# Layer 0's up products of the later chunks as three fp32r terms, and two of layer 1's roundings two slots on

## Time and profile before

| | |
|---|---|
| executions, us | 623.47, 627.16, 627.70 |
| median, us | 627.16 |
| profiled execution: span from first to last instruction, us | 622.5 |
| PE busy in it, us | 601.4 (97%) |
| PE weight loads busy, us | 562.2 (90%) |
| DVE, ACT, POOL busy, us | 345.9, 287.3, 111.0 |
| share of the last-ending chain: PE, DVE, ACT | 83%, 10%, 3% |
| granted clock of TensorE, mean | 0.995 |

### The profile page before, as it was taken

How to read it: one execution, slowest core, us unless ns; L and a number is a source line. 1 busy time by engine, 2 the same in 40 slices (tenths; PEclk the granted TensorE clock), 3 DMA queues, 4 the chain that set the end, 5 groups by cost and what they waited for, 6 DMA issues and landing times.

```text
span 622.5 us, 12422 instructions
## 1 busy us (share of the span) xinstructions
PE 601.4 (97%) x4526; PEld 562.2 (90%) x4526; DVE 345.9 (56%) x1221; ACT 287.3 (46%) x955; POOL 111.0 (18%) x328
## 2 busy tenths in 40 slices
PE   8889999999999999999999999999999999999896
PEld 7678788889999999999999999999989899898895
DVE  4865655765464454455553563158947764766314
ACT  3275645645655455455564556546813332311110
POOL 3034121111111111111111110000201321412310
PEclk8999999999999999999999999999999999999899
DMA  8998000000000000000000000090202002003000
GB/s 260 338 311 134 2 1 2 2 2 1 2 2 1 2 1 2 2 2 1 2 1 1 2 2 2 19 185 15 91 1 103 6 5 103 5 5 107 5 1 8
DMA packets 47477, 26.98 MB, mean 43 GB/s; under 512 B 28424, under 2 KB 42680, under 8 KB 46904
## 3 DMA queue, kind: packets, MB, share of 16 engines
q1 hardware_dynamic: 45392, 25.71, 15.2%
q10 hardware_dynamic: 2024, 0.48, 0.4%
HBM read 25.61 MB, written 0.57 MB: 42 GB/s over the span
## 4 chain that ended last, share of the span: by engine, by line
PE 83%; DVE 10%; ACT 3%; issue 2%; POOL 0%; DVEq 0%; POOLq 0%
PE Y L1371 33%; PE U L1371 30%; PE HH L1371 8%; PE ZR L1371 7%; PE M L1371 5%; DVE acc_a L814 2%; ACT gated L648 1%; DVE acc_b L814 1%; DVE rh L814 1%; DVE rank L846 1%; DVE cmp_a L806 0%; DVE fresh L814 0%; ACT cand L626 0%; POOL scaled_lo L566 0%; DVE cmp_b L806 0%
## 5 line engine op out<-in xcount | busy, mean ns | idle before, releaser
L1371 PE MATMUL Y<-l_dn,gated 128*128 128x128 f32 x1152 | 162.7, 284 | 1.8 <-DVE acc_a L814 0.9
L1371 PEld LDWEIGHTS Y<-l_dn,gated 128*128 128x128 f32 x1152 | 141.1, 192 | 3.3 <-issue 2.0
L648 ACT ACTIVATE gated<-U,b1T 128x256 f32<-128x256 f32 x256 | 106.8, 473 | 0.0
L1371 PE MATMUL U<-l_x_hi,l_up_hi 128*128 128x256 f32 x256 | 82.8, 323 | 0.0
L630 ACT ACTIVATE h<-ZR,rnn_b 128x8 f32<-128x8 f32 x128 | 34.3, 268 | 90.5 <-PE ZR L1371 88.1
L814 DVE SCALAR_TENSOR_TENSOR fresh<-zr_s,cand 128x8 f32<-128x8 f32 x128 | 21.4, 167 | 94.6 <-ACT cand L626 92.1
L1371 PE MATMUL U<-l_x_hi,l_up_lo 128*128 128x256 f32 x256 | 72.0, 281 | 0.0
L1371 PE MATMUL U<-l_x_lo,l_up_hi 128*128 128x256 f32 x256 | 72.0, 281 | 0.0
L550 POOL TENSOR_SCALAR zh<-zr_s 128x8 f32<-128x8 f32 x128 | 25.8, 202 | 251.5 <-ACT zr_s L622 251.5
L626 ACT ACTIVATE cand<-HH 128x8 f32<-128x8 f32 x128 | 22.7, 178 | 96.3 <-PE HH L1371 96.3
L1371 PE MATMUL U<-scaled_hi,l_up_hi 128*128 128x256 f32 x192 | 58.8, 306 | 1.7 <-POOL scaled_lo L566 1.7
(11 more groups left out here) (263 smaller groups left out, 1201.5 us busy)
## 6 DMA issues: line engine op xcount, KB each, us to landing
l_bc<-dw SPq DMA_DIRECT2D x4, 1536.0 KB, 6.4
stage<-L_ffn_W_dram SPq DMA_DIRECT2D x4, 768.0 KB, 10.8
w_raw<-L_ffn_W_dram SPq DMA_DIRECT2D x12, 256.0 KB, 6.6
l_up_raw<-L_ffn_W_dram SPq DMA_DIRECT2D x1, 2048.0 KB, 10.0
l_up_raw<-L_ffn_w_dram SPq DMA_DIRECT2D x1, 2048.0 KB, 14.8
l0f_up<-L_ffn_w_dram SPq DMA_DIRECT2D x1, 768.0 KB, 7.0
l0f_dn<-L_ffn_w_dram SPq DMA_DIRECT2D x1, 768.0 KB, 8.4
x<-x_dram SPq DMA_DIRECT2D x1, 512.0 KB, 4.2
```

The costliest lines, as they stand in the source:

```text
L648: last = nc.scalar.activation(gated[:, n % 4, h * N:(h + 1) * N], U[n % 2][:, h * N:(h + 1) * N], ACT.Gelu, bias=b1T[:, col:col + 1])
L1371: return nc.tensor.matmul(out, lhsT, rhs, start=start, stop=stop, skip_group_check=shared)
```

## The change

Chunks 2 and 3 of stream C, and chunks 1 to 3 of stream F, take their up products as three fp32r terms (`mm3`), as layers 1 and 2 do; the first chunks stay float32. These are 12 C units and 18 F units. For that:

- ScalarE makes six rounded weight parts of 128 x 512 in slots 3, 4, 5, 10, 11 and 12 (`l0_high_part`);
- GpSimd makes the six lo parts (`l0_low_part`), each in the place of the raw weights, so after these were read last, and the hi and lo parts of xT for chunks 2 and 3 early on; layer 1's eight lo parts are woven with them, the last four between the keep steps of GRU steps 0 to 3;
- VectorE makes, at chunk 1, 2 and 3's `take_sums`, a hi and a lo part of the scaled sum ahead of c0, for which it still makes the float32 copy (the router and the order of the rest use it);
- TensorE waits for these parts at the first units that use them;
- layer 1's first two hi parts move from slots 8 and 9 to 10 and 12.

```diff
--- before.py
+++ after.py
@@ -59,8 +59,12 @@
 SIG_SLOT = [AT["C", 5, k] + 5 for k in range(CHUNKS)]
 SIG_SLOT[2] = AT["C", 5, CHUNKS - 1] + 1
 SIG_LATE = SIG_SLOT[1]
+L0_SPLIT_X = CHUNKS - 2
+L0_LAST_RAW = [AT["C", 1, 1], AT["C", 3, 1], AT["F", 1, 0], AT["F", 3, 0], AT["F", 5, 0], AT["C", 5, 1]]
+L0_HI_SLOTS = [3, 4, 10, 11, 12, 5]
+L0_HI_ORDER = sorted(range(6), key=lambda j: L0_HI_SLOTS[j])
 GELU_AGAIN = AT["F", 5, 1], A_START - 2
-UP_HI_SLOTS = [8, 9] + [14 + e for e in range(E - 2)], [A_START + 4 + 2 * e for e in range(E)]
+UP_HI_SLOTS = [10, 12] + [14 + e for e in range(E - 2)], [A_START + 4 + 2 * e for e in range(E)]
 W1_SLOTS = [AT[stream, i, k] for k in (1, 2) for stream, i in zip("AAABBB", (7, 9, 11, 7, 9, 11))]
 
 
@@ -241,6 +245,12 @@
 
         with ExitStack() as raw:
             stage = sb("stage", [P, E3 * F], scope=raw)
+            with ExitStack() as first:
+                l0_w13_hi = sb("l0_w13_hi", [P, 2, 2 * P], F32R, scope=first)
+                l0_up_hi = sb("l0_up_hi", [P, E, P], F32R, scope=first)
+                l0f_up_hi = sb("l0f_up_hi", [P, 12 * P], F32R, scope=first)
+                l0_x = [sb(f"l0_x{i}", [P, 2, N], F32R, scope=first) for i in range(2)]
+                l0f_x = [sb(f"l0f_x{i}", [P, 2, N], F32R, scope=first) for i in range(2)]
             l3_up_turned = sb("l3_up_turned", [P, E3, F], scope=raw)
         l3_up_hi = sb("l3_up_hi", [P, E3, F], F32R)
         l3_up = (l3_up_hi, sb("l3_up_lo", [P, E3, F], F32R))
@@ -271,15 +281,20 @@
 
 
         with ExitStack() as early:
-            l0_up = sb("l0_up", [P, E, P], scope=early)
+            with ExitStack() as raw:
+                l0_up = sb("l0_up", [P, E, P], scope=raw)
+                l0_w13 = sb("l0_w13", [P, 2, 2 * P], scope=raw)
+            l0_up_lo = sb("l0_up_lo", [P, E, P], F32R, scope=early)
+            l0_w13_lo = sb("l0_w13_lo", [P, 2, 2 * P], F32R, scope=early)
             l0_dn = sb("l0_dn", [P, E, D], scope=early)
-            l0_w13 = sb("l0_w13", [P, 2, 2 * P], scope=early)
             l0_w2 = sb("l0_w2", [P, 2, D], scope=early)
             silu = sb("silu", [P, 512], scope=early)
             act = sb("act", [P, 512], scope=early)
             gru_c = sb("gru_c", [P, 3 * D], scope=early)
             relu = sb("relu", [P, 2, 512], scope=early)
-            l0f_up = sb("l0f_up", [P, 12 * P], scope=early)
+            with ExitStack() as raw:
+                l0f_up = sb("l0f_up", [P, 12 * P], scope=raw)
+            l0f_up_lo = sb("l0f_up_lo", [P, 12 * P], F32R, scope=early)
             l0f_dn = sb("l0f_dn", [P, 12, D], scope=early)
             gru_w = sb("gru_w", [P, 3, D], scope=early)
             gru_u = sb("gru_u", [P, 3, D], scope=early)
@@ -353,6 +368,7 @@
         e_full, ga_full, gd_full = sem("e_full"), sem("ga_full"), sem("gd_full")
         l3_hid = sem("l3_hid")
         set_up = sem("set_up")
+        l0_hi, l0_lo, l0_x_split, l0f_x_split = sem("l0_hi"), sem("l0_lo"), sem("l0_x_split"), sem("l0f_x_split")
         l0_sig, silu_done = sem("l0_sig"), sem("silu_done")
         gru_zr, gru_gates, gru_rh = sem("gru_zr"), sem("gru_gates"), sem("gru_rh")
         gru_hh, gru_cand, gru_h, gru_keep = sem("gru_hh"), sem("gru_cand"), sem("gru_h"), sem("gru_keep")
@@ -420,6 +436,17 @@
 
             return (scaled_all, POOL_FIRST.index(j) + 1) if j in POOL_FIRST else (scaled_odd, (j - 1) // 2)
 
+        def l0_weights(tiles, j):
+
+            w13, w_up, f_up = tiles
+            if j == 0:
+                return w13[:, :, :].rearrange("p i n -> p (i n)")
+            if j in (1, 5):
+                return w_up[:, at(4 * (j == 5), 4), :].rearrange("p e h -> p (e h)")
+            return f_up[:, at(512 * (j - 2), 512)]
+
+        l0_raw, l0_high, l0_low = (l0_w13, l0_up, l0f_up), (l0_w13_hi, l0_up_hi, l0f_up_hi), (l0_w13_lo, l0_up_lo, l0f_up_lo)
+
         def bank_of(*name):
 
             return M[m_of(*name) % 2]
@@ -523,6 +550,20 @@
                                    base=0, pattern=[[1, n], [-1, n]], channel_multiplier=0).then_inc(consts, 1)
 
 
+            pool.wait_ge(x_rest, 2)
+            for i in range(2):
+                src = xT[:, at((L0_SPLIT_X + i) * N, N)]
+                own(nc.gpsimd.tensor_copy(l0_x[i][:, 0, :], src))
+                nc.gpsimd.tensor_tensor(out=l0_x[i][:, 1, :], in0=src, in1=l0_x[i][:, 0, :], op=ALU.subtract).then_inc(l0_x_split, 1)
+
+            def l0_low_part(j):
+
+                pool.wait_ge(l0_hi, L0_HI_ORDER.index(j) + 1)
+                pool.wait_ge(u_full, L0_LAST_RAW[j] + 1)
+                nc.gpsimd.tensor_tensor(out=l0_weights(l0_low, j), in0=l0_weights(l0_raw, j), in1=l0_weights(l0_high, j),
+                                        op=ALU.subtract).then_inc(l0_lo, 1)
+
+            l0_low_part(0)
             pool.wait_ge(m_free, m_of("mid", 1) + 1)
             pool.wait_ge(zeros, 5)
             own(nc.gpsimd.tensor_tensor(out=pair_bias[:, 3 * D:], in0=pair_bias[:, 3 * D:], in1=cond_pair[:, :], op=ALU.add))
@@ -534,13 +575,24 @@
             nc.gpsimd.tensor_scalar(gru_u[:, 2, :], gru_u[:, 2, :], 0.5, None, ALU.mult).then_inc(gru_scaled, 1)
 
             pool.wait_ge(gru_scaled, 1)
-            for e in range(E):
+
+            def l1_low_part(e):
+
                 pool.wait_ge(up_hi, e + 1)
                 if e:
                     pool.wait_ge(up_split[0], e)
                 nc.gpsimd.tensor_tensor(out=l1_up_lo[:, e, :], in0=l1_up_raw[:, e, :], in1=l1_up_hi[:, e, :],
                                         op=ALU.subtract).then_inc(up_split[0], 1)
-            pool.wait_ge(up_split[0], E)
+
+            l0_low_part(1)
+            l1_low_part(0)
+            l0_low_part(2)
+            l1_low_part(1)
+            l0_low_part(3)
+            l0_low_part(4)
+            l1_low_part(2)
+            l0_low_part(5)
+            l1_low_part(3)
 
             def gru_keep_of(step):
                 h = h_gru[:, at((step - 1) % (2 * CT) * B, B)]
@@ -552,6 +604,8 @@
 
             for step in range(T):
                 gru_keep_of(step)
+                if step < E - 4:
+                    l1_low_part(4 + step)
 
             pool.wait_ge(y_full, DOWNS.index(AT["F", 5, CHUNKS - 1]) + 1)
             for t in (spread[:, :, :], third[:, :, :]):
@@ -691,6 +745,17 @@
                         if l == 1:
                             sc.wait_ge(y_full, DOWNS.index(AT["C", 5, CHUNKS - 1]) + 1)
                     nc.scalar.activation(up[l][0][:, e, :], (l1_up_raw, l2_up_raw)[l][:, e, :], ACT.Copy).then_inc(up_hi, 1)
+
+            def l0_high_part(n):
+                if n in L0_HI_SLOTS:
+                    j = L0_HI_SLOTS.index(n)
+                    if j == 0:
+                        sc.wait_ge(ld_w13, 16 * W13_LOADS)
+                    if j == 1:
+                        sc.wait_ge(ld_l0, 16 * L0_LOADS)
+                    if j == 2:
+                        sc.wait_ge(ld_l0f, 16 * L0F_LOADS)
+                    nc.scalar.activation(l0_weights(l0_high, j), l0_weights(l0_raw, j), ACT.Copy).then_inc(l0_hi, 1)
 
             def scaled_first_high(j):
                 sc.wait_ge(weighted_full, j + 1)
@@ -740,6 +805,7 @@
                     if quarter == 3 and n != SIG_LATE:
                         square_l0(n)
                     if quarter == 3:
+                        l0_high_part(n)
                         up_high(n)
             for n in range(A_START, SLOTS):
                 steps, rnn = gru_steps(n), rnn_steps(n)
@@ -1052,7 +1118,12 @@
                 if (stream, i, k) == ("C", 5, 0):
                     dve.wait_ge(m_free, m_of("mid", 2) + 1)
                 if (stream, i) == ("C", 5):
-                    ts(c0[k % 2][:, :], taken("c", k)[:, 0:N], 1.0 / 3.0, ALU.mult).then_inc(m_free, 1)
+                    m = taken("c", k)[:, 0:N]
+                    if k:
+                        parts = l0f_x[k % 2]
+                        own(ts(parts[:, 0, :], m, 1.0 / 3.0, ALU.mult))
+                        stt(parts[:, 1, :], m, 1.0 / 3.0, parts[:, 0, :], ALU.mult, ALU.subtract).then_inc(l0f_x_split, 1)
+                    ts(c0[k % 2][:, :], m, 1.0 / 3.0, ALU.mult).then_inc(m_free, 1)
                 if (stream, i) == ("F", 5):
                     tt(x1[:, at(k * N, N)], xT[:, at(k * N, N)], taken("f", k)[:, 0:N], ALU.add).then_inc(m_free, 1)
                 stream, i, k = unit(n - 5)
@@ -1491,8 +1562,15 @@
                         cols = at((2 * i + h) % Q * P, P)
                         last = mm3(u, [w[:, i // 2, cols] for w in up[stream == "B"]],
                                    [x[:, :] for x in (l1_x, l2_x)[stream == "B"]], True, True)
+                    elif stream == "F" and k:
+                        cols = at((2 * i + h) * P, P)
+                        last = mm3(u, [w[:, cols] for w in (l0f_up_hi, l0f_up_lo)], [l0f_x[k % 2][:, side, :] for side in range(2)], True, True)
                     elif stream == "F":
                         last = mm(u, l0f_up[:, at((2 * i + h) * P, P)], c0[k % 2][:, :])
```

(14 more changed lines are left out.)

## The result

The changed kernel took 655.8 us (median; 650.9 to 660.5), the kernel before 625.3 beside it: ratio 1.050 [1.046, 1.053]. The forecast of 627.7 and its range of 622 to 631 were wrong, and every case of the prediction with them: the highest rival stood at 630.9. The ratios leave out executions over 1.5% longer than the shortest of the same kernel, which show a lower granted clock; the medians and the clocks in the table keep them.

A forecast was written before the change was run, and what follows sets the result against it. It took the GRU recurrence to be as much the bound as TensorE in slots 20 to 43. Terms -0.3 - 0.6 - 0.3 - 0.4 + 0 + 0.2 + 0.3 + 1.6 gave +0.5 on 627.16: 627.7 us, range 622 to 631.

The forecast's parts named there:

- the highest rival: Slots 7 to 23: GpSimd's new work slows VectorE, 0.17 us an overlap; 630.9 us, chance 0.14.
- the first part of the change: Three fp32r terms per float32 half, 0.08 us less each; in slots 20 to 43 mostly more waiting, -0.3 us.
- Three terms: Shorter TensorE halves: -0.3 us in slots 18 and 19, -0.6 in 60 to 63, -0.3 in 20 to 43.
- Roundings moved: Slot 8: ScalarE's wait for the l1_dn load goes, so the first F unit and all behind come earlier, -0.4 us.
- ScalarE's hi parts: Slots 3 to 5 and 10 to 12: six new roundings fit in gaps or cover, cost 0, at most 1.2 us.
- GpSimd's lo parts: Subtractions slow overlapping VectorE operations by 0.17 us each; +0.2 early on, +0.3 between keep steps of GRU steps 0 to 3.
- The third rival: Slots 7 to 23: GpSimd's subtractions slow VectorE at many overlaps of 0.17 us; 630.9 us, chance 0.14.
- The splits: Slots 21, 33 and 39: two VectorE operations ahead of c0 delay fresh and the gate products, +1.6 us.
- TensorE sets the time throughout: GRU stretch: the loop shortens with TensorE's work, so the saving counts in full; 622.2 us, chance 0.12.
- half a record: All 60 halves: each term costs half a float32 record, if the loop gives way too; 620.3 us, chance 0.03.
- The landing of l1_dn: Slot 8: a late load makes the slower runs and the change removes that; 624.0 us, chance 0.13.
- The sign that the prediction named for its third rival: A GRU stretch longer than before by over 3 us would show GpSimd's work slowing VectorE.

The follow-up runs named there:

- e13: Changed kernel with layer 0's lo parts subtracted by VectorE and layer 1's subtractions ahead of the keep steps; 657.4 us, ratio 1.045.
- e14: As e13, with the first of the three terms issued twice in slots 20 to 43; 628.2 us, ratio 1.006.
- e1: Kernel before with only layer 1's first two roundings moved to slots 10 and 12; 626.1 us, ratio 1.0024.
- e5: Changed kernel with float32 products from rounded weights, no GpSimd layer-0 or x subtractions, layer 1's ahead of the keep steps; 625.2 us, ratio 1.0024.
- e10: Changed kernel with layer 1's subtractions ahead of the keep steps and the first term issued twice in slots 20 to 43; 637.9 us, ratio 1.019.
- e2: Changed kernel with all parts still made, but float32 products from the rounded weights; 637.5 us, ratio 1.020.
- e7: Changed kernel with all three terms from existing hi parts, without GpSimd's layer-0 subtractions or VectorE's splits; 647.8 us (637.4 to 667.2).
- e8: As e7, with the first term issued twice, four records a half; 626.2 us, ratio 1.003.
- e4: Kernel before, float32, with the 30 units' up products on 192 of 256 columns; 639.8 us, ratio 1.000 from four of ten executions.

## Why the prediction was wrong

**What failed** is the first part of the change, in the sentence "In most steps it only turns into more waiting for rh or h_gru". The half did get 0.08 us shorter, and the loop did stay the bound: 29.0 us against 29.1 for thirteen steps. But the waiting isn't free. It was costed at -0.3 with 0 as its bound on the other side; it measured +24 to +29 (e13 against e14), since with less to stream in each step TensorE loses half its clock and is then slower than the loop, 3.4 to 4.4 us a step against 2.0 to 3.1. No part and no rival had the granted clock in it, though a PEclk line stands on the page of before. The bound of 0 had no row behind it; it took for granted that more slack can't hurt. The waits for rh and h_gru, which the prediction expected to grow from 10 to 12 to 14 us, shrank to 4.3.

Point by point:

1. *Three terms.* Slots 18 and 19: a unit takes 1.60 us (53.18 to 54.78) where the float32 unit of slot 16 takes 1.75; -0.15 a unit, as said. From the start of slot 60 to that of slot 64: 12.42 us (205.55 to 217.97) against 12.86 before: -0.4, said -0.6. Slots 20 to 43: above.
2. *Roundings moved.* In e1 the wait went and the F unit came 0.41 earlier, as predicted, and it was lost two slots on (in the changed kernel this unit starts at 34.20, behind a first short fall of the clock at 30.2). "In slots 10 to 14 one overlap goes and one comes" was the wrong sentence: two came, and held VectorE for 1.0 and 0.6 us. Net, e1: +0.2%, not -0.4 us.
3. *ScalarE's hi parts* cost little. e5, which has them, the splits and x's copies, is 0.24% [0.04, 0.43] over before.
4. *GpSimd's lo parts.* +0.5 forecast, 10 to 12 us measured where the terms don't cover it (e14 to e10; e5 to e2). The third rival had the right place and, in "small operations may wait for a whole one", the right mechanism, but priced each overlap at the 0.17 of the earlier trace rows, an overlap with the last 0.30 us of a subtraction; 0.8 to 1.0 is what a fresh, cmp_b or relu paid. Even at that price the overlaps come to a few us: up to the GRU's step 1 the changed kernel is 2.9 behind e7, which lacks them (59.02 and 56.07), short falls of the clock included. The rest is the clock in the GRU's steps. That a long list of subtractions also makes GpSimd's own keep late (e10, above) was in no part.
5. *The splits.* 0.42 for each of the two operations, near the 0.42 and 0.46 taken:

```profile
L876 DVE TENSOR_SCALAR l0f_x<-M x3: 425/425/425, 65.7 to 150.3; 128x256 fp32r<-128x256 f32 x3
L880 DVE SCALAR_TENSOR_TENSOR l0f_x<-M,l0f_x x3: 424/424/425, 66.1 to 150.8; 128x256 fp32r<-128x256 f32 x3
```

   At full clock steps 1 to 32 took 72.0 us with them (e14) and 70.9 without (e8): +1.1, said +1.6.

Of the rivals, "TensorE sets the time throughout" is refuted by the thirteen steps above; "half a record" by the 0.15 a unit. The landing of l1_dn wasn't what makes slower runs: e1 has the room and isn't faster. The sign that the prediction named for its third rival, a GRU stretch longer by over 3 us, did appear (103.9 against 70.2), for another reason than the rival's.

What stays open: what sets off a single fall (that of 30 us, that of 44), why e4 falls in some executions and not in others and e7's take from 637.4 to 667.2 us, and the 1.7 to 3.7 us that e8 and e14 keep over before at a full clock. A kernel that pads its GRU steps by other means than a repeated product wasn't tried, nor one with float32 products beside VectorE's lo parts, for which e14 stands in.

## What to carry to other kernels

Where a recurrence paces TensorE, its filler work is also what keeps its clock: before making that work cheaper, read the granted clock by stretch, and give "TensorE drops to 1.2 GHz" a price among the rivals (here half speed for 85 us and +5%). After such a change look at the clock line before any wait, because a busy share of 100% looks the same at either level. And don't place a GpSimd instruction with two SBUF inputs beside short VectorE operations that something waits for; count each overlap at the rest of GpSimd's instruction, and look how late the last of a list of them ends.
